# A two-layer gated-attention and expert kernel: order of the attention's fills, of the prologue, of the tail's scores and of the experts' begin

## The reference, cut to what matters

```python
x = x + tanh(g_xattn[0]) * wkv(layernorm(x), ctx)                # L0 attention: a scan over 128 tokens
x = x + tanh(g_ffn[0])   * ffn(layernorm(x))                     # L0 gated FFN, 256 -> 704 -> 256
x = x + tanh(g_xattn[1]) * cross_attention(layernorm(x), ctx)    # L1: 16 heads of 8, softmax over 256
x = x + tanh(g_ffn[1])   * moe(layernorm(x))                     # L1: 8 experts (352 wide) and a shared one
```

## Time and profile before

| | us |
|---|---|
| median of 3 runs (lowest to highest) | 538.46 (537.72 to 539.44) |
| the profiled execution's own time | 537.95 |
| its span, first to last instruction | 536.2 |
| PE busy | 478.7 (89%) |
| DVE busy | 378.2 (71%) |
| ACT busy | 245.8 (46%) |
| POOL busy | 229.4 (43%) |
| mean granted TensorE clock | 0.986 |

### The profile page before, as it was taken

The page is one execution under the profiler, slowest core; times in us unless marked ns, Lnnn a source line. Parts: engine busy times, 40 slices in busy tenths (PEclk is TensorE's granted clock), DMA queues, the critical chain, the costliest instruction groups (busy, mean ns, idle before and its releaser), DMA issues. The chain is left out here.

```text
span 536.2 us, 10408 instructions
## 1 busy us (share of the span) xinstructions
PE 478.7 (89%) x3384; PEld 264.1 (49%) x3384; DVE 378.2 (71%) x768; ACT 245.8 (46%) x478; POOL 229.4 (43%) x303
## 2 busy tenths in 40 slices
PE   2969999999889888999989999987989999899994
PEld 2654574654733533333333333332434655788882
DVE  4987969789658978988888899995635734323231
ACT  2642323221222067888888889877611001123331
POOL 2752334134438446666666666412010370033424
PEclk9987999999999999999999999999999999999998
DMA  6746700000255436666655566600013125269753
GB/s 209 223 162 141 137 2 0 1 0 1 60 140 145 127 77 172 168 157 160 150 147 145 147 160 176 167 9 5 2 62 100 41 101 174 74 162 206 187 132 39
DMA packets 67256, 59.95 MB, mean 112 GB/s; under 512 B 10049, under 2 KB 62257, under 8 KB 67217
## 3 DMA queue, kind: packets, MB, share of 16 engines
q1 hardware_dynamic: 63424, 55.24, 38.5%
q0 software_dynamic: 3072, 4.21, 4.6%
q10 hardware_dynamic: 720, 0.00, 0.1%
HBM read 38.90 MB, written 22.50 MB: 115 GB/s over the span
## 5 line engine op out<-in xcount | busy, mean ns | idle before, releaser
L1201 DVE TENSOR_REDUCE MX<-psum 128x2 f32<-128x512 f32 x256 | 161.2, 683 | 20.2 <-PE psum L1078 19.7
L1241 ACT ACTIVATE HP<-psum 128x512 f32<-128x512 f32 x256 | 138.2, 603 | 38.7 <-PE psum L1092 36.9
L1078 PE MATMUL psum<-QKA 60*128 60x256 bf16 x512 | 79.5, 273 | 18.0 <-DVE MX L1201 9.9
L1167 PE MATMUL psum<-HP,VP 128*32 128x256 f32 x1024 | 81.6, 391 | 0.0
L1092 PE MATMUL psum<-QKA 60*128 60x256 bf16 x512 | 77.6, 272 | 3.5 <-ACT HP L1241 3.4
L525 PE MATMUL psum<-space_a,space_w 128*128 128x512 f32 x160 | 74.5, 616 | 1.1 <-ACT space_a L510 0.8
L1078 PEld LDWEIGHTS psum<-QKA 60*128 60x128 bf16 x512 | 34.0, 94 | 73.1 <-DVE MX L1201 55.4
L1766 POOL DMA_INDIRECT out_x<-OE,to_u x16 | 25.0, 1563 | 64.3 <-ACT OE L1809 61.9
L525 PEld LDWEIGHTS psum<-space_a,space_w 128*128 128x128 f32 x160 | 30.2, 196 | 37.9 <-issue 35.4
L538 ACT ACTIVATE space_a<-psum,hgs 128x512 f32<-128x512 f32 (+1 forms) x24 | 15.6, 651 | 70.6 <-PE psum L525 48.1
L189 PE MATMUL psum<-space_a,wsh 128*128 128x512 f32 (+1 forms) x96 | 43.7, 598 | 2.2 <-DVE HS L1945 1.5
(11 more groups left out here) (189 smaller groups left out, 739.5 us busy)
## 6 DMA issues: line engine op xcount, KB each, us to landing
QKA<-stack_scr SPq DMA_DIRECT2D x32, 480.0 KB, 4.7
stack_scr<-PARTS SPq DMA_DIRECT2D x32, 192.0 KB, 3.0
WE<-in_W SPq DMA_DIRECT2D x16, 352.0 KB
stack_scr<-PARTS SPq DMA_DIRECT2D x32, 128.0 KB, 2.6
XD<-dispatched SPq DMA_DIRECT2D x8, 258.0 KB, 3.7
X<-in_x SPq DMA_DIRECT2D x4, 512.0 KB, 5.8
CTX<-in_ctx SPq DMA_DIRECT2D x4, 512.0 KB, 7.8
MB<-in_mask SPq DMA_DIRECT2D x16, 128.0 KB, 5.6
```

The source lines that it names most:

```text
L1078: return pe.matmul(to[:, tt * T:(tt + 1) * T], QKA[rows, k, 0, h, tt * P:(tt + 1) * P], QKA[rows, k, 1, h, :], start=True, stop=True)
L1167: last = pe.matmul(PVB[32 * j:32 * j + 32, (m // 2) * T:(m // 2 + 1) * T], VP[:, k, st, turned_head(i, m), :], PT[:, i % 2, st, m, :], sta ...
L1201: dve.tensor_reduce(MX[:, par, head_of(n), :], src[:, :].rearrange("p (a s) -> p a s", a=2), axis=AX.X, op=ALU.max).then_inc(a_red, 1)
L1241: act.activation(PT[:, i % 2, st, 2 * half:2 * half + 2, :].rearrange("p j t -> p (j t)"), TBK3[THIRDS[m]], ACT.Exp).then_inc(a_exp, 1)
```

## The change

It has five parts.

1. **Prologue.** X of group 1 is loaded ahead of ctx of group 0. The gates no longer stand among the transfers that ACT waits for first (SP loads them later, and tanh of them comes after keys-and-values unit 9). DVE makes the decay steps DEC while POOL takes the power; PE's mask transposes move behind two units. POOL takes both DEN sums, then both NUM sums, then the quotients, and only then scales the down weights (L848), which stood ahead of the quotients. DVE leaves scan SA of half 0 of group 1 until after the second layer norm. That layer norm signals each tile, PE transposes tile by tile, and the two copies to ZT run one on ACT and one on DVE.
2. **SP's order in a batch.** Before: maxima's store, first half of the fill, maxima's fill, second half. After: first half, maxima's store, second half, maxima's fill.
3. **Batches 14 and 15.** The turned scores of a slot go into a pair of adjoining banks, (2, 3) and (4, 5) in turn, and one exponential of 1024 columns replaces two of 512. The layer norm's statistics of groups 0, 1, 2 move from tail slots 3, 4, 5 to 0, 1, 4, the transposes from slots 9 to 14 to 7 to 12. Of group 3 the first three tiles are normalised in slots 16 and 17, and the last tile's statistics are taken in slot 21.
4. **Experts' begin.** The shared expert's last first-layer matmul of group 0, its tanh of two pieces and the hidden values of piece 0 move ahead of the barrier. After the barrier PE starts with group 1; of group 3 only one tile is left to normalise. Later the first-layer matmuls of group 3 come ahead of `down_shared(2)`, and the first expert's tokens are transposed between `down_shared(2)` and `down_shared(3)`.
5. **Memory.** The shared expert's buffers lie on the keys' and values' (KR, VR), which are kept past the attention; helpers are moved out and take ranges of tiles.

Cut to its core (buffers, renamed semaphores and moved helpers are left out):

```diff
+                ch.eng.tensor_scalar(dst(i), src(i), mv[:, i, 0:1], rstd[:, i:i + 1],
+                                     ALU.subtract, ALU.mult).then_inc(s_tile, 1)
+
+        LN_STEPS = lambda n: n + n
 
...
+                layer_norm_steps(ch, xt_tile(g), lambda i: Z2[:, i, :], GB, s_var2, s_rstd2, g + 1, s_z2)
 
...
+                for b in range(GB):
+                    pe.wait_ge(s_z2, GB * g + b + 1)
+                    for h in range(2):
                         last = pe.transpose(bank[h][:, b * P:(b + 1) * P], Z2[:, b, h * P:(h + 1) * P], ident[:])
-                    last.then_inc(s_z2T, 1)
-
-            def act_zt(act, g):
-                for h in range(2):
+                        if b == GB - 1:
+                            last.then_inc(s_z2T, 1)
+
+            def dve_zt(dve, g, h):
+                dve.wait_ge(s_z2T, 2 * g + h + 1)
+                dve.tensor_copy(ZT[:, h, :], bank[h][:, :]).then_inc(s_zt, 1)
+
+            def act_zt(act, g, hs=(0, 1)):
...
                     load_x(0)
+                    load_x(1, s_xb)
                     load_ctx(0)
-                    load_x(1, s_xb)
...
                              (bqk[:, 0:1], bq), (wq[:], wqT)]
                     assert len(small) == N_SMALL
+                    sp.dma_start(gates[:, 0:2], g_xattn.partition_broadcast(P)).then_inc(s_gates, 16)
+                    sp.dma_start(gates[:, 2:4], g_ffn.partition_broadcast(P)).then_inc(s_gates, 16)
...
-                    act.activation(tg[:], gates[:], ACT.Tanh).then_inc(s_act0, 1)
+                        act.dma_start(td[:], time_decay).then_inc(s_decay, 16)
+                        act.dma_start(tf[:], time_first).then_inc(s_decay, 16)
+                        act.dma_start(bqk[:, 1:2], bk).then_inc(s_bk, 16)
...
+                    act.wait_ge(s_bk, 16)
...
+                        if u == N_TANH:
+                            act.wait_ge(s_gates, 16 * N_GATES)
+                            act.activation(tg[:], gates[:], ACT.Tanh).then_inc(s_act0, 1)
+                    act_zt(act, 0, (0,))
...
-                    pool.wait_ge(s_chain, 16 * N_CHAIN)
+                    pool.wait_ge(s_decay, 32)
                     pool.tensor_scalar(upos[:], tf[:], 0.0, -1.0, ALU.max, ALU.mult).then_inc(s_dv0, 1)
                     pool.tensor_scalar(uneg[:], tf[:], 0.0, None, ALU.min).then_inc(s_dv0, 1)
+                    pool_rstd1(pool, 0)
...
                     for h in range(2):
-                        pool_sums(pool, 0, h)
+                        pool_den(pool, 0, h)
+                    for h in range(2):
+                        pool_num(pool, 0, h)
+                    for h in range(2):
+                        pool_quot(pool, 0, h)
                     pool.wait_ge(s_wts, 96)
                     pool.tensor_tensor(dw[:, :, :], dw[:, :, :], dsb[:, :].unsqueeze(1).broadcast_to([P, NI, C]),
                                        ALU.mult).then_inc(s_dw, 1)
-                    for h in range(2):
-                        pool_quot(pool, 0, h)
+                    power_step(pool, GB, s_var2, s_rstd2, 1)
+                    pool.wait_ge(s_z2, GB)
                     pool_sums(pool, 1, 0)
-                    power_step(pool, GB, s_var2, s_rstd2, 1)
...
 
                     pe_wkv_in(pe, 0, 0)
                     pe_wkv_in(pe, 0, 1, WB2)
-                    pe.wait_ge(s_mask, 32)
-                    for h in range(2):
-                        last = pe.transpose(bank[0][:, h * B:(h + 1) * B], mrow[:, h * P:(h + 1) * P], ident[0:B, 0:B])
-                    last.then_inc(s_mT, 1)
...
                         if u == N_IN:
+                            pe.wait_ge(s_mask, 32)
+                            for h in range(2):
+                                last = pe.transpose(bank[0][:, h * B:(h + 1) * B], mrow[:, h * P:(h + 1) * P], ident[0:B, 0:B])
+                            last.then_inc(s_mT, 1)
                             pe_wkv_in(pe, 1, 0)
...
                     dve_stats1(dve, ch, 0)
-                    dve_z1(dve, 0)
-                    dve_stats1(dve, ch, 1)
-                    dve.wait_ge(s_act0, 3)
+                    dve.wait_ge(s_act0, 2)
                     dve.wait_ge(s_pool0, 10)
                     for h in range(2):
                         ch.do(dve.tensor_scalar(DEC[:, h, :], steps01[:, :, :].rearrange("p b t -> p (b t)"),
                                                 decay[:, h:h + 1], None, ALU.mult))
-                    ch.wait()
+                    dve_z1(dve, 0)
+                    dve_stats1(dve, ch, 1)
                     dve_products(dve, 0, 0)
                     dve_scans(dve, 0, 0)
+                    dve_products(dve, 0, 1, WB2)
+                    dve_scans(dve, 0, 1)
                     dve.wait_ge(s_mT, 1)
                     dve.tensor_copy(maskT[:, :, :].rearrange("p h b -> p (h b)"), bank[0][:, 0:2 * B]).then_inc(s_mT2, 1)
-                    dve_products(dve, 0, 1, WB2)
-                    dve_scans(dve, 0, 1)
                     for h in range(2):
                         dve_recip(dve, 0, h)
                     dve_products(dve, 1, 0)
-                    dve_scans(dve, 1, 0)
+                    dve_scan_b(dve, 0)
+                    dve.wait_ge(s_act0, 3)
                     dve_x1(dve, 0, WB2)
                     dve_ln2(dve, ch, 0)
...
 
+                def tail_pair(b, i, st):
+
+                    return (2, 4)[st], HEADS * b + 4 * i + 2 * st
+
                 def pe_scoresT(pe, g, k, i, st):
 
-                    turned_bank(pe, g, k, i, st, 1)
-                    turned_bank(pe, g, k, i, st, 0)
-                    score_T(pe, k, i, st, 2)
-                    score_T(pe, k, i, st, 0)
-                    score_T(pe, k, i, st, 3).then_inc(a_st, 1)
-                    score_T(pe, k, i, st, 1).then_inc(a_st, 1)
+                    b = GB * g + k
+                    lo, n = tail_pair(b, i, st)
+                    if i == 0 and st == 0:
+                        pe.wait_ge(a_mx[k], 32 * (g + 1))
+                        if b == B - AHEAD_S:
+                            pe.wait_ge(a_red, HEADS * B)
+                    pe.wait_ge(a_exp, n - 2)
+                    score_T(pe, k, i, st, 2, bank[lo + 1])
+                    score_T(pe, k, i, st, 0, bank[lo])
+                    score_T(pe, k, i, st, 3, bank[lo + 1]).then_inc(a_st, 1)
+                    score_T(pe, k, i, st, 1, bank[lo]).then_inc(a_st, 1)
 
                 def pe_both(pe, to_score, to_turn, p):
...
+                    b = GB * g + k
+                    lo, n = tail_pair(b, i, st)
+                    act.wait_ge(a_st, n + 2)
+                    act.wait_ge(a_pv, 8 * b + 2 * i + st - 3)
+                    act.activation(PT[:, i % 2, st, :, :].rearrange("p j t -> p (j t)"),
+                                   psum[:, lo * 512:(lo + 2) * 512], ACT.Exp).then_inc(a_exp, 2)
 
                 def act_exp(act, g, k, i, st):
...
-                SHARED = {(B - 1, 7): [(0, 0)], (B, 0): [(0, 1)], (B, 1): [(1, 0), (1, 1)], (B, 4): [(2, 0)]}
+                STAT4, NORM4 = {0: (0,), 1: (1,), 4: (2,)}, {1: (0,), 4: (1,), 5: (2,)}
+                TURN4, MOST4 = 7, 16
+                SHARED = {(B - 1, 7): [(0, 0)], (B, 0): [(0, 1)], (B, 1): [(1, 0), (1, 1)], (B, 4): [(2, 0)], (B, 5): [(2, 1)]}
                 LAST_STATS = [2, 4, 10, 12, 18]
 
...
                         def sp_batch(g, k):
                             b = GB * g + k
+                            if there(b, 3):
+                                sp_fill(sp, *at(g, k, 3), (0,))
                             if there(b, 1):
                                 sp_max_store(sp, *at(g, k, 1))
                             if there(b, 3):
-                                sp_fill(sp, *at(g, k, 3), (0,))
+                                sp_fill(sp, *at(g, k, 3), (1,))
                             if there(b, 1):
                                 sp_max_fill(sp, *at(g, k, 1))
...
                             if p == 1 and there(b, -1):
                                 act_av(act, b - 1)
-                            if there(b):
+                            if isinstance(b, int) and b == B and p in (2, 5):
+                                tanh_shared(act, 0, p // 3, first=True)
+                            if there(b, AHEAD_S):
                                 act_exp(act, g, k, p // 2, p % 2)
+                            elif there(b):
+                                act_tail_exp(act, g, k, p // 2, p % 2)
...
-                            if tail(b, p) in range(LN4, LN4 + G3):
-                                pool_power4(pool, tail(b, p) - LN4)
+                            for t in STAT4.get(tail(b, p), ()):
+                                pool_power4(pool, tiles_of(t), t + 1)
+                            if tail(b, p) == MOST4:
+                                pool_power4(pool, OTHERS, NG)
                             if p == 0 and there(b, AHEAD_Q):
...
```

(47 more changed lines are left out.)

167 lines of the change are left out of this document (84 added, 83 removed).

## The result

| | before | after |
|---|---|---|
| median of 4 runs each, us | 538.95 (537.72 to 540.39) | 521.67 (520.74 to 523.64) |
| ratio, 95% interval | 1 | 0.9683 (0.9643 to 0.9723) |
| profiled execution: own time, span | 537.95, 536.2 | 522.43, 520.7 |

A forecast was written before the change was run, and what follows sets the result against it. PE was taken to bound the FFN and the end, DVE steady attention. Gains of 4.5 + 4.4 + 2.3 + 2.7 + 1.7 = 15.6 us off 537.95 gave 522.35, median 522.6; range 518.5 to 530.5.

The forecast's parts named there:

- the reciprocal comes only about 1.2 us earlier: Prologue: VectorE, slowed by an added copy and scan and waiting for transposes, starts its reciprocal only about 1.2 us earlier.
- the 4.05 idle us: Prologue, between the two reciprocals: VectorE's 4.05 us of waits for PE, which an earlier PE takes away, with some left.
- Rival A: Prologue: scaling the down weights takes the port before scan SB; VectorE loses 3.4 us, total 526.0; chance 0.13.
- The 5.1: Attention loop: excess of the gaps before slot 0's reduces, 5.1 us in all, of which 4.4 would be gained.
- 1.2 us to spare: Attention loop: the maxima's fill lands near 251, wanted at about 252.2, so it stays hidden with 1.2 us to spare.
- only where a batch's slot 0 opens: Steady attention: VectorE sets the pace and stops only where a batch's slot 0 opens.
- the new wait for the maxima's fill: Batch 15's start: the powers of groups 0 and 1 ahead of the maxima delay their fill, losing 1.7 us.
- the waits of 1.46 and 0.94: Begin of the MoE: PE's waits for hidden values (1.46 us) and ZT4 (0.94) vanish, as both causes move ahead of the barrier.
- The step that the moved matmuls are work in either place: Begin of the MoE: matmuls moved ahead of the barrier are work PE has to do in either place.
- Rival C: Attention loop: maxima come late in every batch behind the fill's halves, 2.4 us times 12 batches, total 547; chance 0.06.
- B: Attention loop: the fill gains little because stores and halves are limited by their transfer; total 526 to 527; chance 0.12.
- D: Whole kernel: two of the five parts don't come, lost in unseen waits; total 528 to 536; chance 0.10.

The follow-up runs named there:

- the run with the constants moved: Changed kernel with VectorE's small constants put into its wait for POOL's layer-norm power and the mask's parts behind the loop over FFN groups: 522.98 us, ratio to before 0.9702.
- Maxima first: Changed kernel with POOL's maxima of batch 15 moved ahead of the two powers of the statistics in batch 14: 521.41 us, ratio to before 0.9652.
- this run's edits: Kernel before with only the begin of the MoE changed, including the earlier statistics and transposes of groups 0 to 2: 536.07 us, ratio 0.9938.
- both runs on the order: Kernel before with SyncE's new order: 532.54 us, ratio 0.9883; changed kernel with the old order put back: 527.13 us, ratio to before 0.9782.

## Why the prediction was right

The time was 0.9 us under 522.6. Part by part, worked out above from the marks:

| part | predicted | measured | range given |
|---|---|---|---|
| prologue | 4.5 | 4.5 | 1.1 to 5.2 |
| SyncE's order | 4.4 | 5.5 | 0 to 5.1 |
| batches 14 and 15 | 2.3 | 2.8 | 0.5 to 4 |
| begin of the MoE | 2.7 | 2.9 | 1.5 to 2.9 |
| experts' begin | 1.7 | 1.9 | 1 to 2.1 |
| sum | 15.6 | 17.5 (of unrounded parts) | |

The third and fourth rows divide the 5.65 us between them by place, as the prediction did: the fourth has the two waits of the earlier trace rows and the barrier, the third all that lies ahead.

The two profiled executions differ by 15.5 us, which agrees with the sum only because their loops were a fast one of before and a slow one of after. The medians give 17.3.

- **Prologue: right in total, two terms wrong against each other.** The step "the reciprocal comes only about 1.2 us earlier" gave 0.35. Its path has the small constants on it, in both kernels; in before `hgu` took 0.17 us (at 38.77), in the changed kernel 1.27, beside POOL's NUM, which now waits for SA. The prediction didn't count that meeting. The other step, that some of the 4.05 idle us "will be left", was wrong the other way: all but 0.36 went. That the equal total is partly luck follows from this. That VectorE sets the pace there is shown by the run with the constants moved: the reciprocal 3.4 us earlier, `pe_wkv_out` 3.4 earlier.
- **Rival A did not come.** SB of group 1 began at 27.29 and took 1.38, the scaling of the down weights (line 895) began at 27.55 and took 4.37 for 3.43 before: POOL waited, not VectorE. The scans beside which NUM no longer runs take 1.22, as the sum had it. By the Trainium skill, "SBUF — State Buffer", section "Who interferes with whom", the first to issue holds the shared pair for its whole instruction; those times and `hgu`'s agree. In the run with the constants moved `hgu` took 0.17 at 32.55 inside POOL's power, drawn from 32.30 to 33.32; that does not fit, unless POOL's start, which is rough, was later.
- **SyncE's order: the mechanism right, the term too small.** SyncE was free to send the first half earlier, and the fill's lateness before slot 0 was what went. The 5.1 that I took as all there is came from one trace with the shortest of four loops. "1.2 us to spare" for the maxima was also an average: in one of the changed kernel's batches their store landed after 5.9 us, and TensorE waited for them. In the same batch and one more the fill itself was late. And VectorE doesn't stop "only where a batch's slot 0 opens": in nearly every batch it waits another 0.6 to 0.7 us for scores before the next reduces (before at 242.50 us, changed kernel at 248.12), which the change left as it was.
- **Batches 14 and 15: right**, 0.5 us more than forecast, with the new wait for the maxima's fill at the place forecast, 1.04 us for 1.7. Maxima first takes it away, so the two powers ahead of them were its cause. What the term did not have is the wait of 0.78 us for YA, which went with the statistics moved to earlier slots.
- **Begin of the MoE: right**, 2.9 us at the upper bound: the waits of 1.46 and 0.94, and the barrier with 0.79 to 0.32. The step that the moved matmuls are work in either place holds: with only this run's edits TensorE is busy 1.9 us more ahead of the barrier (34.51 us for 32.57) and 1.8 less between it and the logits (4.66 for 6.50).
- **Rival C came in single batches**, and often only with the store on ScalarE's queue, where six waits for the maxima cost 6.6 us. **B and D did not come**: B would have left 1 us or less of the order's gain, both runs on the order have 5.5 and more.

## What to carry to other kernels

Cut the traces at marks that every version has, and compare stretches: those outside the loop repeat within 0.02 to 0.5 us where the runs of one kernel scatter by 2 or 3. Size a stretch that scatters from several traces of equal code. Before a gain is put down to a step, compare busy time on both sides of the place: here 0.8 us came from a wait that the statistics' old place had caused, and nothing from the moved matmuls. When a gain is made early, look at what the moved work lands on: the same 1.8 us of small VectorE instructions made TensorE wait 1.2 us in one group and cost nothing to be seen in the wait of another.

## What the runs showed of the hardware

- **A small store beside large transfers.** 24 KB landed in 1.4 to 1.5 us with no 480 KB half ahead, in 3.8 (median) with one ahead on the same queue and in 3.9 (one store) with one ahead on another queue, and in 4.6 to 6.5 with two ahead on another queue. The Trainium skill, "DMA: Bandwidth & Descriptors", section "Two DMAs through the same engine are not ordered", says that descriptors of one queue start in order; I had taken that as the cause of the delay. The delay is there with the store on a queue of its own too, so the order within a queue is not needed for it. What the store shares with the halves was not measured and stays open.
- **The clock with equal code.** The first eight FFN matmuls follow an idle 0.87 us in the changed kernel and 0.88 in the run with maxima first, where nothing up to there differs. Granted clock and busy time of TensorE over them, in the changed kernel and in the other:

```profile
36.20:39.80 3.60, 3.60 (x10) 1.64 (x11) 3.46 (x11) 0.69 (x1) 1.26 (x1) 1.00 0.00 0
```
```profile
36.10:42.80 6.70, 6.70 (x10) 2.80 (x11) 6.49 (x14) 0.69 (x1) 1.27 (x1) 0.54 0.10 11
```

The one ran at 2.4 GHz, the other near 1.2, as before did in the earlier trace rows; so that was not a matter of the gap before them, and what decided it stays open. It cost nothing: `pe_wkv_out` came at 58.09 and 58.03, since VectorE set the pace.
